# Bank products of a linear attention: two row halves of the array with three terms each, in place of packed 128-row products with two terms

## What is computed

```python
h = _layernorm(x) * (1 + ca) + sa
q = (h @ Wq.T)                                   # 16 heads of 32
sigma_q = elu_plus_one(q)
a_unnorm = einsum('bhsd,nhde->nbhse', sigma_q, memories)     # 4 banks n
norm = einsum('bhsd,nhd->nbhs', sigma_q, memory_norms)
a = a_unnorm / clip(norm, EPS)[..., None] * active
combined = einsum('nbhse,hn->bhse', a, softmax(bank_weights))
x = x + ga * (combined @ Wo.T)
# then layer norm, silu(h @ w_gate) * (h @ w_up), the 2 largest of each 4 kept, @ w_down, times gb, added to x
```

## Time and profile before

| | |
|---|---|
| median of 3 runs | 1482.19 us (1480.34 to 1483.12) |
| span of the profiled execution | 1480.5 us |
| PE busy | 1409.1 us (95%), 6634 matmul records |
| DVE busy | 940.5 us (64%) |
| ACT busy | 531.5 us (36%) |
| POOL busy | 553.6 us (37%) |
| `banks_of` matmuls, 512 in all | 68.7 + 64.9 us busy |

### The profile page before, as it was taken

The page is one execution under the profiler, slowest core; times in us unless marked ns, Lnnn a source line. Parts: engine busy times, 40 slices in busy tenths (PEclk is TensorE's granted clock), DMA queues, the critical chain, the costliest instruction groups (busy, mean ns, idle before and its releaser), DMA issues.

```text
span 1480.5 us, 18584 instructions
## 1 busy us (share of the span) xinstructions
PE 1409.1 (95%) x6634; PEld 1166.5 (79%) x6634; DVE 940.5 (64%) x1335; ACT 531.5 (36%) x826; POOL 553.6 (37%) x363
## 2 busy tenths in 40 slices
PE   7989888899888999999999999999999999999997
PEld 6668777778667888888888888778888888888886
DVE  5887889888866455654645457496636455554644
ACT  5547666667453222222212233332222122122221
POOL 0655666565516131332313134553323132232311
PEclk9999999999999999999999999999999999999999
DMA  7302211112341021110202022130202021020102
GB/s 243 114 8 107 85 68 72 60 57 85 143 160 47 0 93 41 51 64 28 92 0 92 28 92 93 56 149 29 93 0 92 11 81 64 28 92 0 64 0 93
DMA packets 24589, 102.71 MB, mean 69 GB/s; under 512 B 3044, under 2 KB 4068, under 8 KB 14828
## 3 DMA queue, kind: packets, MB, share of 16 engines
q1 hardware_dynamic: 24556, 102.31, 18.7%
HBM read 68.73 MB, written 33.57 MB: 69 GB/s over the span
## 4 chain that ended last, share of the span: by engine, by line
PE 71%; DVE 15%; issue 7%; ACT 5%; DMA 1%; POOL 1%; SPq 1%; DVEq 0%; ACTq 0%
PE bank L1095 22%; PE bank L1096 22%; PE bank L1097 22%; DVE banks_r L919 2%; PE bank L1123 2%; ACT sigma_st L551 1%; DVE ln_raw L765 1%; DVE x_ring L886 1%; DVE h_abs L1047 1%; ACT h_full L535 1%; DVE one_each L1035 1%; DVE attn_scaled L881 1%; PE bank L1170 1%; DVE pair_lo L1029 1%; DVE inv_norm L911 1%
## 5 line engine op out<-in xcount | busy, mean ns | idle before, releaser
L1010 DVE TENSOR_TENSOR h_act<-bank,silu_g 128x512 f32<-128x512 f32 x128 | 88.1, 690 | 405.0 <-PE bank L1097 384.3
L451 POOL TENSOR_TENSOR hs_lo<-h_abs,hs_hi 128x512 fp32r<-128x512 f32 x128 | 174.7, 1394 | 417.6 <-ACT hs_hi L669 417.6
L407 POOL TENSOR_TENSOR h_lo<-h_raw,h_hi 128x512 fp32r<-128x512 f32 x64 | 125.1, 1983 | 238.7 <-ACT h_hi L652 238.7
L1095 PE MATMUL bank<-h_hi,gate_w_hi 128*128 128x512 f32 x512 | 200.6, 392 | 7.9 <-ACT silu_g L675 4.5
L1095 PE MATMUL bank<-h_hi,up_w_hi 128*128 128x512 f32 x512 | 200.7, 392 | 7.8 <-DVE h_act L1010 6.0
L1095 PE MATMUL bank<-down_w_hi,hs_hi 128*128 128x512 f32 x512 | 200.0, 391 | 2.4 <-POOL hs_lo L451 2.4
L669 ACT ACTIVATE hs_hi<-h_abs 128x512 fp32r<-128x512 f32 x128 | 74.9, 627 | 350.4 <-DVE h_abs L1047 218.1
L1096 PE MATMUL bank<-h_lo,up_w_hi 128*128 128x512 f32 x512 | 200.1, 391 | 0.0
L1097 PE MATMUL bank<-h_hi,gate_w_lo 128*128 128x512 f32 x512 | 200.0, 391 | 0.0
L1097 PE MATMUL bank<-h_hi,up_w_lo 128*128 128x512 f32 x512 | 199.9, 390 | 0.0
L1096 PE MATMUL bank<-h_lo,gate_w_hi 128*128 128x512 f32 x512 | 199.9, 390 | 0.0
(11 more groups left out here) (131 smaller groups left out, 2544.3 us busy)
## 6 DMA issues: line engine op xcount, KB each, us to landing
h_raw<-h2T_scratch SPq DMA_DIRECT2D x16, 1024.0 KB, 4.8
x_ring<-in_x_dram SPq DMA_DIRECT2D x8, 1024.0 KB, 4.8
x_scratch<-x_ring SPq DMA_DIRECT2D x8, 1024.0 KB, 3.9
h2T_scratch<-h_full SPq DMA_DIRECT2D x8, 1024.0 KB, 3.9
over_x<-x_scratch SPq DMA_DIRECT2D x8, 1024.0 KB, 4.8
acc_scratch<-over_x SPq DMA_DIRECT2D x8, 1024.0 KB, 3.9
over_x<-acc_scratch SPq DMA_DIRECT2D x8, 1024.0 KB, 4.8
out_dram<-over_x SPq DMA_DIRECT2D x8, 1024.0 KB, 3.9
```

The source lines that it names most:

```text
L407: nc.gpsimd.tensor_tensor(h2_lo[:, k], h2_raw[:, k], h2_hi[:, k].bitcast(F32), ALU.subtract).then_inc(h2_lo_done, 1)
L451: nc.gpsimd.tensor_tensor(hs_lo[:, j], h_abs[:, j], hs_hi[:, j].bitcast(F32), ALU.subtract).then_inc(hs_lo_done, 1)
L1010: nc.vector.tensor_tensor(h_act[:, cc, j], bank[2 * (j % 2) + 1][:], silu_g[:, j % 2], ALU.mult).then_inc(h_done, 1)
L1095: nc.tensor.matmul(out_, stat[0], mov[0], start=start, stop=False)
```

## The change

`sigma_hi` and `sigma_lo` are kept unpacked, 128 partitions (4 heads) each. ACT makes `sigma_hi` with one copy for a group in place of two, POOL makes the whole `sigma_lo` with one subtraction for a group as before (now of 128 partitions), and DVE's `sigma_low` is gone with its semaphore. The memories of a pair stand on their own 64 partitions, so `mem_hi`, `mem_lo` have half the columns, and `mem_swapped`, its two loads and its 16 copies are gone. In `banks_of` a matmul contracts 64 rows, one pair of heads, at the row position of that pair: 24 matmuls of 256 columns (groups, three terms, two pairs; the pairs alternate, and write two different PSUM banks). A bank now holds one pair of heads of two groups, so banks are waited for and released two at a time, and `scale_banks` writes through a view with one more dimension.

```diff
@@ -90,9 +90,10 @@
-            sigma_st = sba("sigma_st", [P, 2 * K, T], F32R)
-            mem_hi = sba("mem_hi", [P, K, NB * P], F32R)
-            mem_lo = sba("mem_lo", [P, K, NB * P], F32R)
+            sigma_hi = sba("sigma_hi", [P, K, T], F32R)
+            sigma_lo = sba("sigma_lo", [P, K, T], F32R)
+            mem_hi = sba("mem_hi", [P, K, NB * HALF], F32R)
+            mem_lo = sba("mem_lo", [P, K, NB * HALF], F32R)
...
@@ -255,10 +254,6 @@
                 load_mod(CA, wmod_sb[:, 1])
                 sp.dma_start(norm_raw[:], norm_hd.rearrange("(k p) n -> p k n", p=P)).then_inc(norm_in, 16)
                 sp.dma_start(mem_raw[:], mem_hd.rearrange("(k p) n e -> p k n e", p=P)).then_inc(norm_in, 16)
-                for half in range(2):
-                    sp.dma_start(mem_swapped[HALF * (1 - half):HALF * (2 - half)],
-                                 mem_hd.rearrange("(k p) n e -> p k n e", p=P)[HALF * half:HALF * (half + 1)]
-                                 ).then_inc(norm_in, 16)
                 sp.dma_start(bank_sb[:], bank_w.partition_broadcast(P)).then_inc(norm_in, 16)
                 sp.dma_start(banks_r[0][:].rearrange("p a b c -> p a (b c)"),
                              wqT.rearrange("(k p) n -> p k n", p=P)).then_inc(wq_in, 16)
...
@@ -390,8 +385,8 @@
...
                 for g in range(K):
-                    pool.wait_ge(sigma_hi_done, 8 * t + 2 * g + 1)
-                    nc.gpsimd.tensor_tensor(sigma_st[HALF:, 2 * g], sigma[:HALF, g], sigma_st[:HALF, 2 * g].bitcast(F32),
+                    pool.wait_ge(sigma_hi_done, 4 * t + g + 1)
+                    nc.gpsimd.tensor_tensor(sigma_lo[:, g], sigma[:, g], sigma_hi[:, g].bitcast(F32),
                                             ALU.subtract).then_inc(sigma_lo_done, 1)
                 pool.wait_ge(sigma_lo_done, 4 * t + 4)
...
@@ -547,8 +542,7 @@
             def sigma_high(t, g):
                 act.wait_ge(sigma_done, 4 * t + g + 1)
-                for i, rows in enumerate((slice(0, HALF), slice(HALF, P))):
-                    nc.scalar.activation(sigma_st[rows, 2 * g + i], sigma[rows, g], ACT.Copy).then_inc(sigma_hi_done, 1)
+                nc.scalar.activation(sigma_hi[:, g], sigma[:, g], ACT.Copy).then_inc(sigma_hi_done, 1)
             def sigma_all(t, first=False, between=lambda: None):
                 sigma_exp(t, 0, first)
...
@@ -813,22 +800,21 @@
...
-            mem_bd = xn2[:].rearrange("p k (b n h e) -> p k b n h e", b=PAIR, n=NB, h=PAIR)
+            mem_bd = xn2[:, :, 0:NB * HALF].rearrange("p k (n h e) -> p k n h e", n=NB, h=PAIR)
             norm_cols = norm_bd[:].rearrange("p k n h -> p k (n h)").rearrange(
                 "p k (b n h) -> p k b n h", b=PAIR, n=NB)
             for hh in range(HG):
                 rows = slice(DH * hh, DH * hh + DH)
                 pair, h = hh // PAIR, hh % PAIR
                 for k in range(K):
-                    nc.vector.tensor_copy(mem_bd[rows, k, pair, :, h, :], mem_raw[rows, k])
-                    nc.vector.tensor_copy(mem_bd[rows, k, 1 - pair, :, h, :], mem_swapped[rows, k])
+                    nc.vector.tensor_copy(mem_bd[rows, k, :, h, :], mem_raw[rows, k])
                 ins = nc.vector.tensor_copy(norm_cols[rows, :, pair, :, h], norm_raw[rows])
             ins.then_inc(mem_bd_ready, 1)
             dve.wait_ge(wa_hi, 1)
...
@@ -858,12 +844,9 @@
...
-            nc.vector.tensor_tensor(mem_lo[:], xn2[:], mem_hi[:].bitcast(F32), ALU.subtract).then_inc(gate_ready, 1)
+            nc.vector.tensor_tensor(mem_lo[:], xn2[:, :, 0:NB * HALF], mem_hi[:].bitcast(F32), ALU.subtract).then_inc(gate_ready, 1)
             for g in range(K):
                 sigma_of(0, g)
-                if g > 0:
-                    sigma_low(0, g - 1)
-            sigma_low(0, K - 1)
             for i in range(2):
                 dve.wait_ge(gates_mm, i + 1)
...
@@ -913,13 +896,16 @@
                 nc.vector.tensor_tensor(inv, inv, bank_gate[:].rearrange("p k n h -> p (k n h)"),
                                         ALU.mult).then_inc(r_done, 1)
                 dve.wait_ge(r_done, u + 1)
+                scaled = banks_r[s % 2][:].rearrange("p k n c -> p (k n c)").rearrange(
+                    "p (g i b a e) -> p g i b a e", g=2, i=2, b=PAIR, e=DH)
+                r = inv.rearrange("p (g i b a) -> p g i b a", g=2, i=2, b=PAIR)
                 for g in range(K):
                     dve.wait_ge(banks_done, 4 * u + g + 1)
-                    r = inv[:, g * NB * HG:(g + 1) * NB * HG]
                     nc.vector.tensor_tensor(
-                        banks_r[s % 2][:, g].rearrange("p n (h e) -> p (n h) e", h=HG),
-                        bank[g][:].rearrange("p (a e) -> p a e", e=DH),
-                        r.unsqueeze(2).broadcast_to([P, NB * HG, DH]), ALU.mult).then_inc(banks_r_done, 1)
+                        scaled[:, g // 2, :, g % 2],
+                        bank[g][:].rearrange("p (i a e) -> p i a e", i=2, e=DH),
+                        r[:, g // 2, :, g % 2].unsqueeze(3).broadcast_to([P, 2, NB * PAIR, DH]),
+                        ALU.mult).then_inc(banks_r_done, 1)
             def tile(t, x_wait=None, first=False, last=False):
                 u = 4 * t
...
@@ -942,24 +928,17 @@
                 elif last:
                     for g in range(K):
                         sigma_of(t, g)
-                        if g > 0:
-                            sigma_low(t, g - 1)
-                    sigma_low(t, K - 1)
                 else:
                     sigma_of(t, 0)
                     x_wait()
                     stats(0)
                     sigma_of(t, 1)
-                    sigma_low(t, 0)
                     stats(1, 2, 3)
                     dve.wait_ge(bn1_done, 4 * t + 8)
                     sigma_of(t, 2)
-                    sigma_low(t, 1)
                     ln_aggregate(t + 1, 0, ag1_done)
                     ln_variance(0)
                     sigma_of(t, 3)
-                    sigma_low(t, 2)
-                    sigma_low(t, 3)
                 if not first:
                     attn_rest(t - 1, 2, u - 2, between=lambda: combT_low(u - 1, 1))
...
@@ -1157,19 +1136,23 @@
             def banks_of(t, s):
                 u = 4 * t + s
-                for g in range(K):
+                toks = slice(s * P, (s + 1) * P)
+                for two in range(2):
                     if s == 0:
-                        pe.wait_ge(sigma_lo_done, 4 * t + g + 1)
-                        pe.wait_ge(sigma_lo_dve, 4 * t + g + 1)
+                        pe.wait_ge(sigma_lo_done, 4 * t + 2 * two + 2)
                     else:
-                        pe.wait_ge(banks_r_done, 4 * u - 3 + g)
-                    for pair in range(PAIR):
-
-                        cols = slice(pair * T // PAIR, (pair + 1) * T // PAIR)
-                        stat = sigma_st[:, 2 * g + pair, s * P:(s + 1) * P]
-                        nc.tensor.matmul(bank[g][:, cols], stat, mem_hi[:, g, cols], start=True, stop=False)
-                        ins = nc.tensor.matmul(bank[g][:, cols], stat, mem_lo[:, g, cols], start=False, stop=True)
-                    ins.then_inc(banks_done, 1)
+                        pe.wait_ge(banks_r_done, 4 * u - 2 + 2 * two)
+                    for i in range(2):
+                        g = 2 * two + i
+                        cols = slice(i * T // 2, (i + 1) * T // 2)
+                        for stat, mov, first, last in ((sigma_hi, mem_hi, True, False), (sigma_lo, mem_hi, False, False),
+                                                       (sigma_hi, mem_lo, False, True)):
+                            for pair in range(PAIR):
+                                rows = slice(HALF * pair, HALF * (pair + 1))
+                                ins = nc.tensor.matmul(bank[2 * two + pair][:, cols], stat[rows, g, toks],
+                                                       mov[rows, g], start=first, stop=last)
+                                if i == 1 and last:
+                                    ins.then_inc(banks_done, 1)
             def comb_transpose(u, first=False):
                 pe.wait_ge(comb_done, u + 1)
```

More of the change, by code:

```diff
@@ L113, in adaln_kernel @@
             ones = sba("ones", [P, P])
-            mem_swapped = sba("mem_swapped", [P, K, NB, DH])
             norm_raw = sba("norm_raw", [P, K, NB])
@@ L188, in adaln_kernel @@
             "q_done", "exp_done", "neg_done", "sigma_done", "sigma_hi_done", "sigma_lo_done"))
-        sigma_lo_dve = sem("sigma_lo_dve")
         norm_done, clip_done, recip_done, r_done = map(sem, ("norm_done", "clip_done", "recip_done", "r_done"))
@@ L579, in _ @@
             act.wait_ge(mem_bd_ready, 1)
-            nc.scalar.activation(mem_hi[:], xn2[:], ACT.Copy).then_inc(wa_hi, 1)
+            nc.scalar.activation(mem_hi[:], xn2[:, :, 0:NB * HALF], ACT.Copy).then_inc(wa_hi, 1)
             act.wait_ge(bank_shifted, 1)
@@ L796, in sigma_of @@
```

(4 more changed lines are left out.)

## The result

The changed kernel takes 1454.65 us in the median of 4 runs (1452.15 to 1457.62), the kernel before 1482.65 beside it: ratio 0.9814, 95% interval 0.9802 to 0.9826, 28 us faster. The forecast was 1464 and the range began at 1456: right in sign, 9 us off, and just outside the range.

A forecast was written before the change was run, and what follows sets the result against it. DVE and PE were taken to bound phase A in turn: six loop tiles -15.0, last -2.2, first -0.6, sum -17.8 from the 1480.5 us span gives 1462.7. The median stands 1.7 higher, so 1464 us; range 1456 to 1502.

The forecast's parts named there:

- DVE stretch and PE stretch in turn: Loop tile 5: chain through ACT and DVE from about 217 to 246 us, then PE alone from 246 to 262.
- the -3.2 at `combT_lo`: Loop tile: DVE 3.2 us ahead, 1.9 from the sigma and 1.3 from the last subtraction and ACT's second copies.
- X: PE's time for one subtile's bank products: 2.0 us before, taken as 2.4 after, bounds 1.65 and 4.6.
- load and stream in turn within a half: Bank products: both halves together, 12 x (0.073 + 0.11) + 0.2 = 2.4 us per subtile.
- rival 1: Bank products: halves together, weight loads hidden, 1.65 us per subtile; 25 us gained, 1457 us; chance 0.16.
- +0.4 for the fourth subtile: PE stretch: the one subtile's bank products on the chain cost 2.4 - 2.0 = 0.4 us more per tile.
- Second norms 0.3 late: DVE stretch: PE delivers second norms at 235.4 against DVE's need at 235.1, cutting the 3.2 us gain to 2.9.
- First tile: Setup and first tile: -1 us for 16 copies gone and smaller memory splits, +0.4 for its fourth subtile; -0.6 in all.
- Last tile -2.2: Last tile: `combT_lo` can start at 362.7 instead of 364.90, 2.2 us gained; its PE stretch is covered by DVE waits.
- Phase B as long as before: Phase B: nothing in it is touched, so it costs the same, 0 us.
- -22.4 for the removed work: DVE's and ACT's removed work: 3.2 us in each of six loop tiles, 2.2 in the last, 1 in the first.
- +4.6 for the products' form: Half-row products: 0.3 us for late norms and 0.4 for the fourth subtile in six tiles, 0.4 in the first.

The follow-up runs named there:

- e4_act_dve: Changed kernel with ACT's two sigma copies for one and DVE's four spare subtractions per tile put back: 1477.27 us.
- e10_all_but_products: Changed kernel with ACT's second copies, DVE's subtractions and the setup's two loads and 16 copies put back, leaving only the half-row products: 1478.54 us, 0.9979 of the kernel before.
- e3_dve: Changed kernel with DVE's four subtractions per tile put back at their old places, into a spare tile nobody reads: 1475.65 us.

## Why the prediction was right or wrong

- **What bounds the kernel: right.** DVE stretch and PE stretch in turn, and the removed work in the DVE stretch on the path. Its worth, the -3.2 at `combT_lo`, was 3.0 in the trace and 2.8 when put back.
- **X, the step that failed.** I took 2.4 us, "load and stream in turn within a half", from 4-row records that start 0.073 apart. Measured: 1.63, rival 1. A pair comes each 0.12 us with 256 columns and each 0.112 with 128, so 0.073 + 0.11 was never to be added. The 4-row records stream 4 columns: they have nothing to hide a load behind, so they could not tell whether loads are hidden, and the row nearest in kind was the packed matmul's 0.12. The Trainium skill, "TensorE: Matmul & The Clock Gate", part 3, says that matmuls on different row groups run at the same time; by that rule X is the lower bound, and the trace agrees with 1.63. The sum had +0.4 for the fourth subtile of six tiles and of the first, and it measured -0.37: 0.77 x 7 = 5.4 us, more than half of the 9.8 by which 17.8 missed the 27.6 between the spans.
- **Second norms 0.3 late: wrong**, and it followed from X. With 1.63 nothing is late, and `combT_lo` to `t1` kept its 13.4 us. That is 1.8 us more.
- **First tile: mis-sized.** The term was -0.6 and measured -5.1. I said that the copies lie "beside q products and gates", but DVE's `mods`, on which the first h waits, stand behind them: loads and copies 2.0 and DVE's and ACT's work in this tile 1.7 (`e4_act_dve`'s `t1` at 60.73), 3.2 when both are put back (`e10_all_but_products`), and the products' form 1.9 where I had +0.4. I had applied the loop's findings to six tiles and the last, and not to the first.
- **Last tile -2.2: right**, -2.6 measured.
- **Phase B as long as before: nearly**, 1020.3 us after the change and 1022.3 before, from the first down projection to the end. The eleven kernels of the experiments, with the same phase B, have 1021.0 to 1022.5, so this isn't the change. 1.4 of the 2.0 us arise at one place. PE waits there for ACT's `silu_g`, and the kernel before has a stretch at the lower clock right behind this wait, the changed kernel one ahead of it, and then a shorter wait (first the kernel before, then the changed one):

```profile
PE bank L1095 <- ACT silu_g L675: 3.4, 1, 3.4
978.00:982.00 4.00, 4.00 (x11) 3.15 (x11) 3.93 (x6) 2.67 (x3) 3.20 (x3) 0.57 0.01 4
```

```profile
907.00:911.00 4.00, 4.00 (x11) 3.14 (x12) 3.86 (x8) 0.22 (x1) 0.00 (x0) 0.57 0.00 0
PE bank L1074 <- ACT silu_g L669: 1.8, 1, 1.8
```

- **The clock: not in the sum.** The 2.0 us in phase B are luck. Against them, the changed kernel lost 3.1 us at the lower clock in two periods of the loop, where the kernel before lost 1.6 in one, and the second tile's `t1` falls into such a stretch in the changed kernel alone (0.9 us, 59.06 to 62.26 where it was 64.16 to 66.49). The two lots of luck roughly cancel.
- **The range.** It gave 0.16 to rival 1 and began at 1456, just under that rival's 1457. The right X alone would have given 1457; the first tile, with -5.1 where rival 1 had -1.4, made most of the rest.

By sums: I had -22.4 for the removed work and +4.6 for the products' form. The whole times of the runs gave -23.9 and -4.1. These two differences share the clock's scatter, but the sign of the second is clear: the interval of `e10_all_but_products` excludes zero, and X fell by 0.37 in the trace. Nearly the whole miss is this sign.

## What to carry to other kernels

Two matmuls of half the rows on the two halves of the array cost one (0.12 us here), if they alternate in the instruction stream; in blocks of twelve they cost nearly the full sum (2.60 us for 24, where 24 in turn would be 2.9). A price taken from very short matmuls says what isn't hidden there, and nothing on whether it is hidden beside long ones. Work that is removed in each tile is removed in the first one too, where it may stand ahead of everything: read the setup's own waits.

## What I had not expected of the hardware

- TensorE started work for the idle half when three matmuls of the other were left, not one and not twelve (0.34 us more at blocks of six, 6 of 24 overlapped at twelve).
- Less work for PE went with a slower kernel: with half the columns of the bank products the granted clock was 0.90 over a tile in place of 1.00, and the tile took 42.3 us in place of 41.0 (one run).
- What a stretch at the lower clock costs hangs on where it falls: in `e3_dve` it lay in the PE stretch and the period was 44.46; with more work for ACT besides it lay in the DVE stretch, and the period was 43.82. In phase B it lay ahead of a wait in the changed kernel, and the wait was 1.8 us in place of 3.4.
